# Moving the clamp and the last factor product of a group-norm, channel-norm and gate kernel from VectorE to GpSimd, with a new order on GpSimd

## The chip, the cores and the metric

The kernel runs on one core of a Trainium2 chip. The time is that of one launch on the device, in microseconds; three runs of the kernel before gave 1960.15, 1960.63 and 1963.23, a median of 1960.63. TensorE (PE) multiplies matrices into PSUM, VectorE (DVE) and ScalarE (ACT) work elementwise on SBUF and PSUM, GpSimd (POOL) elementwise on SBUF, and SyncE (SP) starts the loads. "us" is microseconds.

## The reference

The input `x` is 8 x 128 channels x 256 x 256 pixels in float32. Cut to what is computed:

```python
g = group_norm(x)                       # 32 groups of 4 channels; over the group's channels and all pixels, eps 1e-5
u = mean(g, channels); s = sqrt(var(g, channels, ddof=1))       # one value per pixel
n = (g - u) / (s + 1e-6)
n = einsum('bchw,oc->bohw', n, W) + b   # 128 x 128 matrix over the channels
out = x + g * n
```

## The kernel before, in words

**Layout and tiles.** The 128 channels are the partitions. A batch is 65536 pixels, cut into 64 slots of 1024 pixels (512 KB). Subtracting the channel mean is folded into the centred and turned matrix `w_t`. Since a group's mean and variance run over a whole batch, each batch is read first for its statistics; 33 of its 64 slots stay in SBUF from then on (`tiles`, 49 buffers), the other 31 are loaded a second time ("stream"). All of slots 41 to 63 but none of slots 0 to 10 are among the second loads.

**Stages.** The program has a first stage without output (statistics of batch 0) and then one period of 64 steps for each batch. In step t of a period, PE, DVE, ACT and POOL each do the parts below for slots that lag behind t, and the statistics of the next batch run in between, so that the periods join without a gap. Every engine walks the same steps in a program order that is written out by hand; semaphores tie them.

- **Normalise, POOL L441** (`norm`): one step ahead, `(x - mean) * inv_std`, in place. It waits for a streamed slot's load.
- **Squares, ACT L524**, then **sums, PE L722**: sums over the channels of the tile and of its squares, 32 matmuls a slot. Four slots (a "set") share one accumulator of 128 x 128 sums; there are 16 sets a batch, 128 in all.
- **Once per set**, a chain on 128x128 values turns the sums into the factor 1/(s + eps). In step t = 4 of the set (its first slot is 0): ACT squares the sum (L540, `sum_sq`), DVE forms `var` (L651) and clamps and scales it (L655, `max(var, 1e-30) / 127`). In step 5: ACT root, root + eps and root squared (L527, L529, L530), DVE reciprocal (L663, `approx`), POOL three products (L485, L459, L461) that correct the reciprocal for the error of the root. In step 6: DVE makes the last product (L667, `factor = (miss - 2) * approx`); the factor is split into three bf16 pieces by ACT L533, POOL L466 (`split_first`), ACT L536, POOL L471 (`split_second`).
- **Spread, PE L708**: from step 7 on, one slot a step, the factor is laid out over all partitions in PSUM (`factor_ps`, a single buffer).
- **Scale, DVE L632**: normalised tile times factor, eight steps behind. **Project, PE L734**: `w_t` times that, into one of two PSUM buffers.
- **Gate, DVE L645**: `(proj + shift) * tile`, in place, nine steps behind; **finish, POOL L452** (`finish`) adds the mean in the same step, and ACT starts the store one step later (L548).
- **Statistics of the next batch:** 24 slots go to DVE (two `bn_stats` each, L676 and L677) and 40 to ACT (two passes with an accumulator each, L509), over steps 0 to 57. DVE has places for its slots in the last step of each set only, mostly two slots there, in some sets one.
- **Group scalars, `gn_scalars`, L580 to L618:** in steps 59, 61 and 62, DVE turns the statistics into the scalars of the next batch, in small instructions of one or two columns, each of which waits for the one before.

**Order on each engine, inside one step.** DVE: scale, reciprocal, last factor product, gate, `var` and clamp, statistics, group scalars. POOL: normalise, first split, the three products, finish, second split. ACT: squares, the root group, the piece copies with one statistics pass between them, one statistics pass and then `sum_sq` (`SUM_SQ_AFTER = 1`), the remaining passes, the store. PE: spread, project, sums. SP: loads in the order of a planner that spaces the 95 loads of a batch 0.62 steps apart; each waits until its buffer's last user is done, and for 33 kept and all streamed buffers that is a store.

Of the kernel before, what the change touches and what calls it, by code (L numbers as in the profile page):

```python
# [8 lines left out]
ALU = mybir.AluOpType  # L9
# [3 lines left out]
P = 128  # L13
# [3 lines left out]
TINY = 1e-30  # L17
# [19 lines left out]
LAG_VAR = SPLIT  # L37
# [151 lines left out]
def norm_gate_kernel(nc, x, w, bias, const, pick, ident, out):  # L189
# [23 lines left out]
    with ExitStack() as ctx:  # L213
# [87 lines left out]
        miss_squared = sem("miss_squared")  # L301
        factor_done = sem("factor_done")
# [5 lines left out]
        SUM_SQ_AFTER = 1  # L308
# [118 lines left out]
        def _(pool):  # L427
# [27 lines left out]
            def correct(done):  # L455

                pool.wait_ge(approx_done, done)
                pool.wait_ge(miss_done, done)
                nc.gpsimd.tensor_tensor(miss[:, :], miss[:, :], approx[:, :], ALU.mult).then_inc(miss_scaled, 1)  # L459
                pool.wait_ge(miss_scaled, done)  # L460
                nc.gpsimd.tensor_tensor(miss[:, :], miss[:, :], approx[:, :], ALU.mult).then_inc(miss_squared, 1)  # L461

# [11 lines left out]
            def period(b, own, before, nxt):  # L474
                for step in steps(own, before, nxt):
                    root_of = set_behind(step, LAG_ROOT, b, own, before)
                    fit_of = set_behind(step, LAG_FIT, b, own, before)
                    if (s := behind(step, -NORM_LEAD, own, before, nxt)) is not None:
                        norm(b, step, s, own)
                    if fit_of is not None:  # L480
                        split_first(fit_of)
# [7 lines left out]
                    if fit_of is not None:  # L489
                        split_second(fit_of, step)  # L490
# [62 lines left out]
        def _(dve):  # L553
# [10 lines left out]
            def gn_scalars(n, part, of):  # L564
# [11 lines left out]
                if part == 0:  # L576
# [9 lines left out]
                    then(nc.vector.scalar_tensor_tensor(out=cell(5), in0=cell(4), scalar=cell(4), in1=cell(1),  # L586
                                                        op0=ALU.mult, op1=ALU.add))
                    then(nc.vector.scalar_tensor_tensor(out=cell(4), in0=cell(4), scalar=bn_part, in1=cell(2),
                                                        op0=ALU.mult, op1=ALU.subtract))
                    then(nc.vector.scalar_tensor_tensor(out=cell(5), in0=cell(5), scalar=bn_part, in1=cell(3),  # L590
                                                        op0=ALU.mult, op1=ALU.add))

                    then(nc.vector.scalar_tensor_tensor(out=cell(5), in0=cell(4), scalar=cell(4), in1=cell(5),
                                                        op0=ALU.mult, op1=ALU.subtract))
                    then(nc.vector.tensor_scalar(cell(6), cell(4), pivot_of(of), None, ALU.add))
                elif part == 1:
# [3 lines left out]
                    then(nc.vector.scalar_tensor_tensor(out=cell(7), in0=cell(7), scalar=cell(7), in1=cell(5),  # L600
                                                        op0=ALU.mult, op1=ALU.subtract))
# [3 lines left out]
                else:  # L605
# [3 lines left out]
                    then(nc.vector.scalar_tensor_tensor(out=cell(11), in0=cell(8), scalar=cell(10), in1=cell(9),  # L609
                                                        op0=ALU.mult, op1=ALU.add))  # L610
# [10 lines left out]
            def period(b, own, before, nxt):  # L621
                of = plan if own else first_plan
                for step in steps(own, before, nxt):
# [24 lines left out]
                    def var_of_sums(ready):  # L648
# [5 lines left out]
                        dve.wait_ge(var_sum_done, ready)  # L654
                        nc.vector.tensor_scalar(var[:, :], var[:, :], TINY, 1.0 / (P - 1), ALU.max, ALU.mult)\  # L655
                            .then_inc(var_done, 1)
# [7 lines left out]
                    if (ready := set_behind(step, LAG_FIT, b, own, before)) is not None:  # L664

                        dve.wait_ge(miss_squared, ready)
                        nc.vector.scalar_tensor_tensor(out=factor[:, :], in0=miss[:, :], scalar=-2.0, in1=approx[:, :],  # L667
                                                       op0=ALU.add, op1=ALU.mult).then_inc(factor_done, 1)
# [112 lines left out]
```

## Time and profile before

| | |
|---|---|
| median of 3 runs | 1960.63 us |
| the profiled execution: its own time / its span | 1957.16 us / 1955.4 us |
| granted TensorE clock | 0.992 |
| DVE busy | 1803.2 us (92%) |
| PE busy | 1713.4 us (88%) |
| POOL, ACT busy | 1460.6 us (75%), 1440.7 us (74%) |
| DMA | 671.63 MB, mean 343 GB/s |

The span runs from the first to the last instruction. The first stage ends at 97.5 us, when POOL takes over batch 0's scalars; the eighth and last takeover is at 1711.5 us, so a period with statistics for a next batch takes (1711.5 - 97.5) / 7 = 230.6 us on average. Durations of neighbouring instructions on one engine overlap a little, since the next one begins before the last one has left the pipeline; from start to start is what one costs in a busy row of them.

### The profile page before, as it was taken

What the parts mean: (1) busy time and instruction counts of PE and PEld (TensorE: products, weight loads), DVE (VectorE), ACT (ScalarE), POOL (GpSimd) and SP (SyncE); (2) the same over time, 40 slices, a digit from 0 to 9 for tenths busy, and PEclk for the clock granted to TensorE, in tenths of its full rate; (3) what the DMA queues carried; (4) which work ended last, traced back from release to release, by engine and by line L of the source; (5) the groups of instructions that cost most, each with busy time, mean ns of one, the idle gap of its engine ahead of it and who ended that gap; (6) DMA issues with size and microseconds to landing.
All of it is one profiled execution on the core that took longest, in us unless ns stands there. A gap on an engine that the chain in (4) does not pass through costs nothing.

```text
span 1955.4 us, 67613 instructions
## 1 busy us (share of the span) xinstructions
PE 1713.4 (88%) x28706; PEld 922.9 (47%) x28706; DVE 1803.2 (92%) x2120; ACT 1440.7 (74%) x2498; POOL 1460.6 (75%) x1684
## 2 busy tenths in 40 slices
PE   0079997999889998999989999899988999899997
PEld 0045554555445554455545554455544555455553
DVE  5669999999999998999989998999989999898988
ACT  5598885888768885788858888588876888544442
POOL 0077877878778886788868787787877888688885
PEclk9989999999999999999999999999999999999999
DMA  9989998999989998999989999899998999854775
GB/s 379 390 308 337 388 377 291 402 378 377 337 293 415 372 385 322 338 396 373 387 303 378 372 385 350 304 406 373 380 346 310 401 364 384 315 196 185 270 258 218
DMA packets 184188, 671.63 MB, mean 343 GB/s; under 512 B 20688, under 2 KB 21072, under 8 KB 183888
## 3 DMA queue, kind: packets, MB, share of 16 engines
q1 hardware_dynamic: 110160, 398.85, 55.0%
q10 hardware_dynamic: 73728, 268.47, 34.6%
q8 instruction: 227, 3.72, 0.7%
q14 instruction: 73, 0.60, 0.1%
HBM read 398.80 MB, written 268.44 MB: 341 GB/s over the span
## 4 chain that ended last, share of the span: by engine, by line
PE 47%; DVE 27%; issue 9%; DMA 9%; POOL 3%; SPq 2%; ACT 2%; POOLq 0%; ACTq 0%; DVEq 0%
PE proj_ps L734 28%; PE sums_ps L722 10%; DVE scaled L632 9%; PE factor_ps L708 9%; DMA tiles<-x 6%; DVE tiles L645 6%; DVE bn L676 4%; DVE bn L677 4%; DMA out<-tiles 3%; SPq L408 2%; POOL tiles L441 1%; POOL tiles L452 1%; DVE var L651 1%; ACT unused L509 1%; DVE gn L580 1%
## 5 line engine op out<-in xcount | busy, mean ns | idle before, releaser
L734 PE MATMUL proj_ps<-scaled,w_t 128*32 128x512 f32 x8192 | 992.3, 602 | 0.1
L452 POOL TENSOR_SCALAR tiles<-tiles,out_shift 128x1024 f32<-128x1024 f32 x512 | 576.8, 1127 | 228.6 <-DVE tiles L645 214.9
L645 DVE SCALAR_TENSOR_TENSOR tiles<-proj_ps,gate_shift,tiles 128x1024 f32<-128x1024 f32 x512 | 643.2, 1256 | 46.4 <-PE proj_ps L734 46.0
L441 POOL TENSOR_SCALAR tiles<-tiles,norm_scalars 128x1024 f32<-128x1024 f32 x512 | 618.6, 1208 | 58.0 <-DMA tiles<-x 57.2
L509 ACT ACTIVATE unused<-tiles,bn 128x1024 uint8<-128x1024 f32 x560 | 636.5, 1137 | 2.5 <-issue 1.7
L632 DVE TENSOR_TENSOR scaled<-tiles,factor_ps 128x1024 f32<-128x1024 f32 x512 | 618.4, 1208 | 6.1 <-PE factor_ps L708 3.8
L524 ACT ACTIVATE squares<-tiles 128x1024 f32<-128x1024 f32 x512 | 539.0, 1053 | 99.1 <-POOL tiles L441 74.2
L708 PE MATMUL factor_ps<-pieces,pick_sb 128*128 128x128 bf16 x4096 | 319.8, 221 | 130.5 <-DVE scaled L632 111.5
L722 PEld LDWEIGHTS sums_ps<-tiles,const_sb 128*32 128x32 f32 x8192 | 245.6, 111 | 317.9 <-issue 283.7
L734 PEld LDWEIGHTS proj_ps<-scaled,w_t 128*32 128x32 f32 x8192 | 214.7, 109 | 365.0 <-issue 311.5
L708 PEld LDWEIGHTS factor_ps<-pieces,pick_sb 128*128 128x128 bf16 x4096 | 232.5, 98 | 245.8 <-DVE scaled L632 164.5
L722 PE MATMUL sums_ps<-tiles,const_sb 128*32 128x128 f32 x8192 | 320.1, 274 | 11.9 <-ACT squares L524 11.9
L722 PE MATMUL sums_ps<-squares,const_sb 128*32 128x128 f32 x8192 | 319.7, 274 | 0.0
L722 PEld LDWEIGHTS sums_ps<-squares,const_sb 128*32 128x32 f32 x8192 | 235.8, 111 | 0.3
L533 ACT ACTIVATE piece<-sum_sq,const_sb 128x128 bf16<-128x128 f32 x128 | 51.7, 404 | 155.6 <-DVE sum_sq L667 155.6
L663 DVE RECIPROCAL approx<-approx 128x128 f32<-128x128 f32 x128 | 120.6, 942 | 15.4 <-ACT approx L529 15.4
L655 DVE TENSOR_SCALAR var<-var 128x128 f32<-128x128 f32 x128 | 123.3, 963 | 4.4
L676 DVE BATCH_NORM_STATS2 bn<-tiles 128x6 f32<-128x512 f32 x168 | 114.5, 682 | 0.0
L677 DVE BATCH_NORM_STATS2 bn<-tiles 128x6 f32<-128x512 f32 x168 | 113.7, 677 | 0.0
L459 POOL TENSOR_TENSOR miss<-miss,approx 128x128 f32<-128x128 f32 x128 | 59.1, 462 | 68.2 <-DVE approx L663 66.2
L527 ACT ACTIVATE root<-var 128x128 f32<-128x128 f32 x128 | 39.7, 310 | 92.3 <-DVE var L655 91.6
L509 ACT ACTIVATION_READ_ACCUMULATOR unused<-tiles,bn 128x1 f32 x560 | 106.0, 189 | 0.0
(56 smaller groups left out, 679.9 us busy)
## 6 DMA issues: line engine op xcount, KB each, us to landing
tiles<-x SPq DMA_DIRECT2D x760, 512.0 KB, 9.7
out<-tiles ACTq DMA_DIRECT2D x512, 512.0 KB, 6.9
const_sb<-const SPq DMA_DIRECT2D x1, 193.5 KB, 2.3
scaled<-w SPq DMA_DIRECT2D x1, 64.0 KB, 2.1
scaled<-ident SPq DMA_DIRECT2D x1, 64.0 KB, 2.1
pick_sb<-pick SPq DMA_DIRECT2D x1, 8.0 KB, 2.2
bias_sb<-bias SPq DMA_DIRECT2D x1, 0.5 KB, 2.3
```

Of the source, the lines that this page charges most:

```text
L441: nc.gpsimd.tensor_scalar(place(s), place(s), norm_scalars[:, 0:1], norm_scalars[:, 1:2], ALU.add, ALU.mult).then_inc(normed, 1)
L452: nc.gpsimd.tensor_scalar(place(s), place(s), 1.0, out_shift[:, 0:1], ALU.mult, ALU.add).then_inc(finished, 1)
L509: nc.scalar.activation(unused[:, which, :], data, (ACT.Identity, ACT.Square)[which], bias=pivot_of(of), scale=-1.0, accum_out=act_sums[:, ...
L524: nc.scalar.activation(squares[:, step % 2, :], place(step), ACT.Square).then_inc(squared, 1)
L632: nc.vector.tensor_tensor(scaled[:, s % 2, :], place(s), factor_ps[:, :], ALU.mult)\
L645: nc.vector.scalar_tensor_tensor(out=place(s), in0=proj_ps[:, s % 2, :], scalar=gate_shift[:, 0:1], in1=place(s), op0=ALU.add, op1=ALU.mul ...
L655: nc.vector.tensor_scalar(var[:, :], var[:, :], TINY, 1.0 / (P - 1), ALU.max, ALU.mult)\
L676: nc.vector.bn_stats(bn_of(of)[:, j, :], data[:, 0:BANK])
L677: nc.vector.bn_stats(bn_of(of)[:, j + 1, :], data[:, BANK:SLOT]).then_inc(bn_done, 1)
L708: mm = nc.tensor.matmul(factor_ps[:, chunk(h, t)], pick_sb[:, j:j + 1].to_broadcast([P, P]), pieces[:, s // SPLIT % 2, :], start=True, sto ...
L722: mm = nc.tensor.matmul(sums_of(s)[32 * t:32 * t + 32, which, :], rows, data[:, chunk(h, t)], start=(which == 0 and k == 0), stop=(which = ...
L734: mm = nc.tensor.matmul(proj_ps[q:q + 32, s % 2, h:h + BANK], w_t[:, q:q + 32], scaled[:, s % 2, h:h + BANK], start=True, stop=True)
```

## The change

It moves two 128x128 instructions of each set from DVE to POOL, and reorders POOL's step.

- The clamp L655 becomes a POOL `tensor_scalar` (`clamp`), after normalise in step 4; it waits for `var_sum_done` of DVE.
- The last factor product L667 becomes two POOL instructions at the end of `correct`: `miss * 1.0 - 2.0` and then the product with `approx`. They stand in step 5 instead of step 6.
- POOL's order in a step becomes: normalise, clamp, second split, products, finish, first split. The first split is issued at the end of step 5, where it was after normalise in step 6; the second split comes after normalise in step 6, where it was after finish.
- `SUM_SQ_AFTER` goes from 1 to 0: ACT squares the sum before its first statistics pass of the step, not after it.
- Six one-column `scalar_tensor_tensor` of `gn_scalars` become `tensor_scalar` with two column operands.

No instruction of PE, no load and no store is changed, nor the order of ACT beyond that constant.

```diff
-        SUM_SQ_AFTER = 1
+        SUM_SQ_AFTER = 0
...
                 nc.gpsimd.tensor_tensor(miss[:, :], miss[:, :], approx[:, :], ALU.mult).then_inc(miss_squared, 1)
+                pool.wait_ge(miss_squared, done)
+                nc.gpsimd.tensor_scalar(miss[:, :], miss[:, :], 1.0, -2.0, ALU.mult, ALU.add).then_inc(miss_shifted, 1)
+                pool.wait_ge(miss_shifted, done)
+                nc.gpsimd.tensor_tensor(factor[:, :], miss[:, :], approx[:, :], ALU.mult).then_inc(factor_done, 1)
+
+            def clamp(done):
+
+                pool.wait_ge(var_sum_done, done)
+                nc.gpsimd.tensor_scalar(var[:, :], var[:, :], TINY, 1.0 / (P - 1), ALU.max, ALU.mult).then_inc(var_done, 1)
...
                     if (s := behind(step, -NORM_LEAD, own, before, nxt)) is not None:
                         norm(b, step, s, own)
+                    if var_of is not None:
+                        clamp(var_of)
                     if fit_of is not None:
-                        split_first(fit_of)
+                        split_second(fit_of, step)
                     if root_of is not None:
...
                     if (s := behind(step, LAG_OUT, own, before)) is not None:
                         finish(b, step, s, before)
-                    if fit_of is not None:
-                        split_second(fit_of, step)
+                    if root_of is not None:
+                        split_first(root_of)
...
-                    then(nc.vector.scalar_tensor_tensor(out=cell(5), in0=cell(4), scalar=cell(4), in1=cell(1),
-                                                        op0=ALU.mult, op1=ALU.add))
+                    then(nc.vector.tensor_scalar(cell(5), cell(4), cell(4), cell(1), ALU.mult, ALU.add))
...
                         nc.vector.scalar_tensor_tensor(out=var[:, :], in0=sum_sq[:, :], scalar=-1.0 / P,
                                                        in1=sums_of(step - LAG_VAR)[:, 1, :], op0=ALU.mult, op1=ALU.add)\
                             .then_inc(var_sum_done, 1)
-                        dve.wait_ge(var_sum_done, ready)
-                        nc.vector.tensor_scalar(var[:, :], var[:, :], TINY, 1.0 / (P - 1), ALU.max, ALU.mult)\
-                            .then_inc(var_done, 1)
...
-                    if (ready := set_behind(step, LAG_FIT, b, own, before)) is not None:
-
-                        dve.wait_ge(miss_squared, ready)
-                        nc.vector.scalar_tensor_tensor(out=factor[:, :], in0=miss[:, :], scalar=-2.0, in1=approx[:, :],
-                                                       op0=ALU.add, op1=ALU.mult).then_inc(factor_done, 1)
```

The other five column forms (L588, L590, L593, L600, L609) are changed in the same way as the one shown (L586).

## Rows read from the trace of the kernel before

**Rows 1.** The page: busy times, and the chain that ended last

```profile
PE 1713.4 (88%) x28706; PEld 922.9 (47%) x28706; DVE 1803.2 (92%) x2120; ACT 1440.7 (74%) x2498; POOL 1460.6 (75%) x1684
PE 47%; DVE 27%; issue 9%; DMA 9%; POOL 3%; SPq 2%; ACT 2%; POOLq 0%; ACTq 0%; DVEq 0%
```

**Rows 2.** Timeline of DVE: `var` at sets' starts in batch 2 and the last

```profile
571.19 0.28 DVE L651 SCALAR_TENSOR_TENSOR var<-sum_sq,sums_ps 128x128 f32<-128x128 f32 x1
738.00 0.28 DVE L651 SCALAR_TENSOR_TENSOR var<-sum_sq,sums_ps 128x128 f32<-128x128 f32 x1
803.79 0.28 DVE L651 SCALAR_TENSOR_TENSOR var<-sum_sq,sums_ps 128x128 f32<-128x128 f32 x1
1729.66 0.28 DVE L651 SCALAR_TENSOR_TENSOR var<-sum_sq,sums_ps 128x128 f32<-128x128 f32 x1
1887.10 0.28 DVE L651 SCALAR_TENSOR_TENSOR var<-sum_sq,sums_ps 128x128 f32<-128x128 f32 x1
```

**Rows 3.** Timeline of DVE: one set of four steps with two statistics slots

```profile
654.63 0.28 DVE L651 SCALAR_TENSOR_TENSOR var<-sum_sq,sums_ps 128x128 f32<-128x128 f32 x1
654.95 1.07 DVE L655 TENSOR_SCALAR var<-var 128x128 f32<-128x128 f32 x1
655.94 1.21 DVE L632 TENSOR_TENSOR scaled<-tiles,factor_ps 128x1024 f32<-128x1024 f32 x1
657.07 0.94 DVE L663 RECIPROCAL approx<-approx 128x128 f32<-128x128 f32 x1
...
660.16 0.32 DVE L667 SCALAR_TENSOR_TENSOR sum_sq<-miss,approx 128x128 f32<-128x128 f32 x1
660.40 1.27 DVE L645 SCALAR_TENSOR_TENSOR tiles<-proj_ps,gate_shift,tiles 128x1024 f32<-128x1024 f32 x1
...
668.91 0.28 DVE L651 SCALAR_TENSOR_TENSOR var<-sum_sq,sums_ps 128x128 f32<-128x128 f32 x1
```

**Rows 4.** Lines taken alone: ns min/median/max, first and last start

```profile
L655 DVE TENSOR_SCALAR var<-var x128: 226/1074/1087, 111.4 to 1929.0; 128x128 f32<-128x128 f32 x128
L600 DVE SCALAR_TENSOR_TENSOR gn<-gn x8: 219/1072/1073, 94.5 to 1704.4; 128x1 f32<-128x1 f32 x8
L609 DVE SCALAR_TENSOR_TENSOR gn<-gn x8: 219/714/792, 96.2 to 1709.6; 128x1 f32<-128x1 f32 x8
L586 DVE SCALAR_TENSOR_TENSOR gn<-gn x8: 219/876/877, 92.3 to 1695.4; 128x1 f32<-128x1 f32 x8
L585 DVE TENSOR_SCALAR gn<-gn,bn x7: 213/214/215, 303.4 to 1695.2; 128x1 f32<-128x1 f32 x7
L584 DVE TENSOR_SCALAR gn<-gn x8: 170/1099/1121, 91.9 to 1694.1; 128x2 f32<-128x2 f32 x8
L435 POOL COPY norm_scalars<-new_scalars x8: 186/186/186, 97.5 to 1711.5; 128x2 f32<-128x2 f32 x8
```

**Rows 5.** Timeline of POOL in the set of rows 3

```profile
654.82 1.12 POOL L452 TENSOR_SCALAR tiles<-tiles,out_shift 128x1024 f32<-128x1024 f32 x1 [2.17 <-DVE tiles L645]
655.93 1.21 POOL L441 TENSOR_SCALAR tiles<-tiles,norm_scalars 128x1024 f32<-128x1024 f32 x1
657.09 0.47 POOL L485 TENSOR_TENSOR miss<-var,miss 128x128 f32<-128x128 f32 x1
658.09 0.47 POOL L459 TENSOR_TENSOR miss<-miss,approx 128x128 f32<-128x128 f32 x1 [0.53 <-DVE approx L663]
658.63 0.46 POOL L461 TENSOR_TENSOR miss<-miss,approx 128x128 f32<-128x128 f32 x1
```

**Rows 6.** Windows: length, busy us of PE, PEld, DVE, ACT, POOL; clock, DMA share, GB/s

```profile
0.00:90.00 90.00, 0.77 (x2) 0.50 (x2) 55.58 (x89) 54.61 (x90) 0.21 (x4) 1.00 0.99 393
566.50:740.50 174.00, 164.83 (x2795) 88.62 (x2792) 170.25 (x196) 150.64 (x267) 140.54 (x161) 1.00 1.00 385
595.50:624.50 29.00, 27.97 (x471) 14.77 (x467) 28.14 (x34) 25.69 (x46) 24.58 (x29) 1.00 1.03 417
1730.00:1880.00 150.00, 150.00 (x2568) 81.29 (x2560) 136.22 (x140) 71.69 (x116) 130.41 (x151) 1.00 0.60 227
```

**Rows 7.** Waits in batch 2 (552 to 784 us): total, times, longest

```profile
ACT piece L533 <- DVE sum_sq L667: 18.0, 16, 3.8
PE factor_ps L708 <- DVE scaled L632: 14.1, 23, 2.2
POOL tiles L441 <- DMA tiles<-x: 8.5, 5, 3.3
PE factor_ps L708 <- POOL pieces L471: 4.8, 2, 3.2
DVE var L651 <- ACT sum_sq L540: 1.5, 4, 0.7
```

More of the change, by code:

```diff
@@ L301, in norm_gate_kernel @@
         miss_squared = sem("miss_squared")
+        miss_shifted = sem("miss_shifted")
         factor_done = sem("factor_done")
@@ L475, in period @@
                 for step in steps(own, before, nxt):
+                    var_of = set_behind(step, LAG_VAR, b, own, before)
                     root_of = set_behind(step, LAG_ROOT, b, own, before)
@@ L585, in gn_scalars @@
                     then(nc.vector.tensor_scalar(cell(4), cell(0), pivot_of(of), None, ALU.subtract))
-                    then(nc.vector.scalar_tensor_tensor(out=cell(5), in0=cell(4), scalar=cell(4), in1=cell(1),
-                                                        op0=ALU.mult, op1=ALU.add))
[L588 to L594, printed above, removed]
+                    then(nc.vector.tensor_scalar(cell(5), cell(4), cell(4), cell(1), ALU.mult, ALU.add))
+                    then(nc.vector.tensor_scalar(cell(4), cell(4), bn_part, cell(2), ALU.mult, ALU.subtract))
+                    then(nc.vector.tensor_scalar(cell(5), cell(5), bn_part, cell(3), ALU.mult, ALU.add))
+                    then(nc.vector.tensor_scalar(cell(5), cell(4), cell(4), cell(5), ALU.mult, ALU.subtract))
                     then(nc.vector.tensor_scalar(cell(6), cell(4), pivot_of(of), None, ALU.add))
@@ L599, in gn_scalars @@
                     then(nc.vector.tensor_scalar(cell(7), cell(6), small_ps[:, 0:1], None, ALU.subtract))
-                    then(nc.vector.scalar_tensor_tensor(out=cell(7), in0=cell(7), scalar=cell(7), in1=cell(5),
-                                                        op0=ALU.mult, op1=ALU.subtract))
+                    then(nc.vector.tensor_scalar(cell(7), cell(7), cell(7), cell(5), ALU.mult, ALU.subtract))
                 elif part == 2:
@@ L607, in gn_scalars @@
                     then(nc.vector.reciprocal(cell(10), cell(9)))
-                    then(nc.vector.scalar_tensor_tensor(out=cell(11), in0=cell(8), scalar=cell(10), in1=cell(9),
-                                                        op0=ALU.mult, op1=ALU.add))
+                    then(nc.vector.tensor_scalar(cell(11), cell(8), cell(10), cell(9), ALU.mult, ALU.add))
                     then(nc.vector.tensor_scalar(cell(11), cell(11), 0.5, None, ALU.mult))
```

## The prediction

> **What bounds the kernel now.** I read the busy times and the chain of waits first [rows 1]. DVE is busy for 92% of the span, PE for 88%, and together they hold 74% of the chain; no engine is free enough to say at once which one sets the pace. So I then followed one instruction that comes once per set, DVE's `var`, through the timeline and took the distance from one set to the next [rows 2]. In the last batch, which has no statistics for a next one, 12 sets take 1887.10 - 1729.66 = 157.44 us, 13.12 us each, and PE is busy for 150 of 150 us there, DVE for only 136.2 [rows 6]. That is PE's own pace, 3.28 us a step. In batch 2 the same 12 sets take 738.00 - 571.19 = 166.81 us, 13.90 each, and the last four 803.79 - 738.00 = 65.79 us.
>
> The timeline of DVE shows why the earlier batches are slower [rows 3]. This set takes 668.91 - 654.63 = 14.28 us with DVE in an almost unbroken row of work, and PE waits for DVE's scale, 14.1 us in the batch [rows 7]. DVE's row holds a clamp of 1.07 us on 128x128 values. Its durations lie between 0.226 and 1.087 us with a median of 1.074 [rows 4], and the one shown ends at 656.02, just as POOL's finish, which had begun at 654.82 for 1.12 us, ends at 655.94 [rows 3, 5]. The clamp mostly waits for a POOL instruction that is under way. The same is seen on one-column instructions: L600, L586 and L609 take 0.22 us at best and 1.07, 0.88 and 0.71 in the median [rows 4]. In the main part of a batch DVE is thus the limit, PE is right behind it, and the DMA queues are a third: share 1.00 at 385 GB/s over 174 us [rows 6].
>
> **The change, part by part, for a batch with statistics (seven of eight).**
>
> *Clamp and product leave DVE.* From start to start the clamp costs 655.94 - 654.95 = 0.99 us and the product 660.40 - 660.16 = 0.24 [rows 3], 1.23 us a set. The heavy set of 14.28 us would come to 13.05, just under PE's 13.12. So the 12 sets can gain at most 166.81 - 157.44 = 9.4 us, since PE takes over as the bound at once; the other four can gain 4 x 1.23 = 4.9.
>
> *Column forms.* L600, L586 and L609 fall to what a one-column `tensor_scalar` with a column operand takes, 0.214 us in all of its seven executions (L585): 0.86 + 0.66 + 0.50 = 2.0 us a batch, on DVE alone and late in the batch, where PE has to wait for it. L588, L590 and L593 count nothing, since they seldom wait. A row speaks against this: L584, a `tensor_scalar` of two columns, takes 1.10 us in the median [rows 4]. If the new ones wait like it, the 2.0 are lost. I take 2.0, because L585 has one column, as they do. (The Trainium skill, SBUF — State Buffer, section "Who interferes with whom", says that `tensor_scalar` can enter a two-port mode that locks out GpSimd and is blocked by it, and that two SBUF inputs also contend. By its list of operations alone, without the operands, this term would be 0 and the sum 14 us higher. The trace agrees with it for L584 and not for L585.)
>
> *POOL takes on three instructions.* The product costs what the others do, 658.63 - 658.09 = 0.54 us. Clamp and shift are one-input forms of 128 columns, which no row shows. Below: an eighth of finish's 655.93 - 654.82 = 1.11 us, 0.14. Above: the two-input 0.46. Between a two-column copy of 0.19 and 1.11 at 1024 [rows 4, 5] lies 0.19 + 126 x 0.92 / 1022 = 0.30, which I take, an estimate. The sum is 1.2 us a set with a semaphore gap (0.8 to 1.6). POOL is busy 130.41 us in 150, or 11.4 in 13.12 [rows 6], and comes to 12.6 (12.2 to 13.0), still under PE's 13.12, but with half a microsecond left where it had 1.7. The cost is nothing while that cover holds; if it is gone, see the last rival.
>
> *The clamp's wait on POOL.* It waits for `var`, and finish is queued behind it. Finish already waits for the gate that stands just ahead of `var`, 2.17 us in this set [rows 5], so the wait adds `var` and clamp, 0.6 us, once a set. The root chain behind it gets earlier: clamp's end moves from 656.02 to about 655.3. It could get later by up to one normalise (1.2 us) where POOL is late; then the reciprocal, which DVE reaches one scale (1.13 us) after `var`, waits, and the gate behind it.
>
> *Order and splits.* The products now sit before finish with 0.84 us more ahead of it, so one finish and one store a set start that much later; the buffer has a step of slack for that. The first split is issued a step earlier, the second split ahead of finish, so PE's wait for the pieces (4.8 us, in two instances) can shrink or, since normalise now stands right behind a wait for ACT's copy, turn into a late normalise. I count both as 0 (-2 to +2 a batch). ACT's wait for the factor is 18.0 us over 16 sets [rows 7], slack that covers this.
>
> *`SUM_SQ_AFTER`.* DVE waits 1.5 us a batch for `sum_sq` [rows 7]. At most that is gained; ACT may idle for PE where it ran a pass before. Taken as 0.
>
> *DMA.* Nothing is added, but the same bytes have to come sooner. 174 us at 385 GB/s are 67.0 MB. At the 393 GB/s of the load-only first 90 us that takes 170.5 us, 3.5 less; at the best stretch, 417 over 29 us [rows 6], 160.7, or 13.3 less. So the 12 sets gain between 3.5 (slower rate) and 9.4 (PE). Neither end is nearer to the rows, since the stretch itself holds both kinds of rate, so I take the middle, 6. What the loads owe is paid in the last four sets, where all slots are streamed and normalise already waits 8.5 us for them; there I take half of 4.9 + 2.0, 3.5.
>
> *Elsewhere.* The first stage is loads at a share of 0.99, gain 0. The last batch already runs at PE's pace and gains 0 (up to 5 us worse, if POOL slips by 0.3 a set).
>
> The sum is 7 x (6 + 3.5) = 66.5 off the profiled execution's own 1957.2, 1890.7. The median of the runs lies 3.5 above that execution, so the forecast is 1894 us.
>
> **The rivals.**
>
> *PE's floor is reached.* The loads keep up, and each batch gains 9.4 + 6.9 = 16.3: 7 x 16.3 = 114, or 1847 us. For it speaks that DVE's heavy set comes out at 13.05; against it that four engines and the DMA all lie within a few per cent of 13.12 us and wait for each other in order. (The Trainium skill, HBM Reference, section "Specifications (TRN2)", gives about 425 GB/s for a core that streams alone. By that the 67.0 MB take 158 us and this rival would be the forecast. The rows show 417 for 29 us and 385 for 174.)
>
> *The loads take it back.* If 390 GB/s is all that this mixture reaches, the 12 sets gain 2, and of the last four only 1 is left, because waits for streamed slots grow: 7 x 3 = 21, or 1940 us. For it speak the share of 1.00 and the 8.5 us of waits, against it the 417.
>
> *POOL becomes the bound, slower than before.* Everything on POOL stands in one order, so a wait at the head (clamp for `var`, products for the reciprocal, 0.53 today [rows 5], both splits for ACT's copies) holds back finish and normalise. The seven batches run at 14.54 us a set on average in batch 2 (232.6 / 16), the last at 13.12. With x us a set everywhere the change is 112 (x - 14.54) + 16 (x - 13.12), zero at x = 14.36. That needs 1.7 us of waits on top of 12.6. At x = 14.5 it is +18 us, 1979. Against it speaks that 1.2 us of added work fill 1.7 of slack, and that most waits stand where POOL would otherwise idle.
>
> **How the numbers follow.** The forecast has 0.56, PE's floor 0.14, loads 0.17, POOL 0.09, and that gains and waits cancel 0.04. About 0.2% (4 us) is what a measurement of this kernel can tell from none. Faster is 0.56 + 0.14 + 0.17 = 0.87, the same 0.04, slower 0.09. The forecast's own range is 1865 to 1925. The range reaches to 1942, over the rival of the loads, and down to 1858, most of the way to PE's floor; it leaves out POOL's 0.09 and some 0.1 below.
>
> **What the profile after would show.** Right: L651 at 13.3 to 13.5 us apart in the 12 sets of a middle batch; clamp on POOL at 0.3 us, all alike; the one-column forms at 0.21; DVE busy about 1640 us (1803 - 128 x 1.23 - 7 x 2); POOL about 1610 (1460.6 + 128 x 1.2), at 85%; DMA above 395 GB/s in the 12 sets and longer waits of normalise for loads late in a batch. Wrong: a POOL instruction of 128 columns above 0.5 us; the reciprocal waiting for ACT more than 0.5 us a set; sets of the last batch above 13.4 us; PE waiting for pieces in most sets; or 13.12 in all 12 sets, in which case the loads were no limit.

## The result, and the profile after

The changed kernel takes 1931.41 us in the median of four runs (1927.35 to 1935.11) against 1960.72 of the kernel before, a ratio of 0.986 with a 95% interval of 0.983 to 0.989. It is faster by 29 us, 1.4%, and the interval is clear of 1; I had forecast 66. The profiled execution is the slowest of the four, 1935.11 us with a span of 1933.3, against 1957.16 and 1955.4.

The page of the changed kernel, busy times and the chain that ended last, as in [rows 1]:

```profile
PE 1714.7 (89%) x28706; PEld 923.1 (48%) x28706; DVE 1646.0 (85%) x1864; ACT 1441.0 (75%) x2498; POOL 1631.2 (84%) x2068
PE 33%; POOL 22%; DVE 18%; issue 10%; ACT 8%; DMA 6%; SPq 2%; ACTq 0%; POOLq 0%; DVEq 0%
```

DVE lost 157 us of work, nearly what was forecast, and the span lost 22. POOL and ACT are in the chain now, with 22% and 8% where they had 3% and 2%. So work went away from DVE, and waiting came in its place.

Timeline of DVE in the changed kernel, `var` (now L658) at the same places as [rows 2]:

```profile
566.14 0.28 DVE L658 SCALAR_TENSOR_TENSOR var<-sum_sq,sums_ps 128x128 f32<-128x128 f32 x1
733.26 0.28 DVE L658 SCALAR_TENSOR_TENSOR var<-sum_sq,sums_ps 128x128 f32<-128x128 f32 x1
795.49 0.28 DVE L658 SCALAR_TENSOR_TENSOR var<-sum_sq,sums_ps 128x128 f32<-128x128 f32 x1
1707.53 0.28 DVE L658 SCALAR_TENSOR_TENSOR var<-sum_sq,sums_ps 128x128 f32<-128x128 f32 x1
1866.83 0.28 DVE L658 SCALAR_TENSOR_TENSOR var<-sum_sq,sums_ps 128x128 f32<-128x128 f32 x1
```

The 12 sets take 167.12 us where they took 166.81: nothing was gained in the main part of a batch. The last four take 62.23 where they took 65.79, and that is where the time came from. In the mean over batches 1 to 6 the last four gained 4.0 us a batch, where I had forecast 3.5, and the 12 sets lost 0.3, where I had forecast a gain of 6. In the last batch 12 sets take 159.30 us, 13.28 each, where PE's pace had given 13.12.

The waits of the changed kernel over the whole run (total, times, longest):

```profile
DVE approx L667 <- ACT approx L542: 134.6, 122, 4.2
ACT piece L546 <- POOL sum_sq L466: 126.5, 119, 2.8
PE factor_ps L707 <- DVE scaled L639: 89.3, 104, 3.0
POOL tiles L442 <- DMA tiles<-x: 23.5, 20, 3.1
PE factor_ps L707 <- POOL pieces L481: 13.9, 41, 2.4
```

DVE waits 134.6 us at the reciprocal for root + eps, 1.05 us a set. In the kernel before that wait was 15.4 us in all. The wait of normalise for loads, on which I had put a part of the sum and which I expected to grow, is 23.5 us, and had been 57.2. Most of what it lost is in the set of steps 52 to 55, in which it was 3.39 us a batch before and is 0.39 now (mean over batches 1 to 6).

Two lines of the changed kernel taken alone, POOL's clamp and POOL's shift (ns min/median/max):

```profile
L471 POOL TENSOR_SCALAR var<-var x128: 639/640/643, 110.9 to 1908.3; 128x128 f32<-128x128 f32 x128
L464 POOL TENSOR_SCALAR miss<-miss x128: 298/299/303, 115.4 to 1911.8; 128x128 f32<-128x128 f32 x128
```

The shift costs the 0.30 us that I had estimated for both. The clamp has the same shape but a maximum in it, and costs 0.64, above my upper bound of 0.46.

Timeline of DVE in a set with two statistics slots, which answers to [rows 3]:

```profile
649.25 0.27 DVE L658 SCALAR_TENSOR_TENSOR var<-sum_sq,sums_ps 128x128 f32<-128x128 f32 x1
649.44 1.21 DVE L639 TENSOR_TENSOR scaled<-tiles,factor_ps 128x1024 f32<-128x1024 f32 x1
651.70 0.95 DVE L667 RECIPROCAL approx<-approx 128x128 f32<-128x128 f32 x1 [1.04 <-ACT approx L542]
...
663.38 0.28 DVE L658 SCALAR_TENSOR_TENSOR var<-sum_sq,sums_ps 128x128 f32<-128x128 f32 x1
```

ACT in the same stretch:

```profile
648.85 1.14 ACT L522 ACTIVATE unused<-tiles,bn 128x1024 uint8<-128x1024 f32 x1
649.89 0.20 ACT L522 ACTIVATION_READ_ACCUMULATOR unused<-tiles,bn 128x1 f32 x1
649.99 1.05 ACT L537 ACTIVATE squares<-tiles 128x1024 f32<-128x1024 f32 x1
650.93 0.30 ACT L540 ACTIVATE root<-var 128x128 f32<-128x128 f32 x1
651.27 0.40 ACT L542 ACTIVATE approx<-root,const_sb 128x128 f32<-128x128 f32 x1
```

And POOL's clamp there:

```profile
649.61 0.64 POOL L471 TENSOR_SCALAR var<-var 128x128 f32<-128x128 f32 x1 [0.97 <-DVE var L658]
...
663.74 0.64 POOL L471 TENSOR_SCALAR var<-var 128x128 f32<-128x128 f32 x1 [0.91 <-DVE var L658]
```

DVE is done with scale about 650.66 and stands until 651.70. The clamp ends at 650.25, ACT is in squares until 651.04, root begins at 650.93 and root + eps is there at 651.67. Before, the scale began only when the clamp had ended, and so covered the root chain; now it begins with the clamp and is over before the root has begun. POOL's row from clamp to clamp is 14.13 us with 0.91 of waiting. The other 13.2 us are more than PE's 13.12, though POOL is busy for 12.72 of them only; the rest are gaps between its 16 instructions that are too short to be listed as waits.

There is a second thing in this set, and it was there before as well. PE's spreads around the step with two statistics slots, in the kernel before (L708):

```profile
646.20 0.62 PE L708 MATMUL factor_ps<-pieces,pick_sb 128*128 128x128 bf16 x8
649.48 0.62 PE L708 MATMUL factor_ps<-pieces,pick_sb 128*128 128x128 bf16 x8
653.58 0.62 PE L708 MATMUL factor_ps<-pieces,pick_sb 128*128 128x128 bf16 x8 [0.76 <-DVE scaled L632]
657.20 0.62 PE L708 MATMUL factor_ps<-pieces,pick_sb 128*128 128x128 bf16 x8 [0.27 <-DVE scaled L632]
```

In the changed kernel (L707):

```profile
640.81 0.62 PE L707 MATMUL factor_ps<-pieces,pick_sb 128*128 128x128 bf16 x8
644.13 0.62 PE L707 MATMUL factor_ps<-pieces,pick_sb 128*128 128x128 bf16 x8
648.19 0.62 PE L707 MATMUL factor_ps<-pieces,pick_sb 128*128 128x128 bf16 x8 [0.71 <-DVE scaled L639]
651.47 0.62 PE L707 MATMUL factor_ps<-pieces,pick_sb 128*128 128x128 bf16 x8
```

A step is 3.28 us. Before, two steps were long, 4.10 and 3.62. Now one is, 4.06, while the other is 3.28: the second was the clamp's, the first was not. DVE in that step of the changed kernel:

```profile
643.35 1.28 DVE L652 SCALAR_TENSOR_TENSOR tiles<-proj_ps,gate_shift,tiles 128x1024 f32<-128x1024 f32 x1 [0.28 <-PE proj_ps L733]
644.55 0.68 DVE L675 BATCH_NORM_STATS2 bn<-tiles 128x6 f32<-128x512 f32 x1
...
646.34 0.67 DVE L676 BATCH_NORM_STATS2 bn<-tiles 128x6 f32<-128x512 f32 x1
646.93 1.20 DVE L639 TENSOR_TENSOR scaled<-tiles,factor_ps 128x1024 f32<-128x1024 f32 x1
```

It is a loop: DVE's gate waits for PE's project (0.28 us here), then come gate (1.20), two slots (2.38) and scale (1.2), and only then, at 648.19, may PE spread again. From the gate's start to that spread are 4.84 us. PE's spread before it came 0.78 us after the gate's start, at 644.13, and 4.84 - 0.78 is the step of 4.06. DVE can't run ahead through this loop, since it starts with a wait for PE. In batch 2 the kernel before has eight steps of 4.10 and eight of 3.62 in the 12 sets, 8 x 0.82 + 8 x 0.34 = 9.3 us of the 9.4 over PE's pace. In the changed kernel the eight steps with two slots take 3.84 to 4.10, the 3.62 are gone, and other steps have grown instead, to as much as 4.24.

### The profile page after: what moved, and what is told of

Its sections match the earlier page's. It is cut to its first block, busy times and chain, and to the rows that moved or that the text cites. A ratio compares the mean times of both kernels' runs of the same rounds, so it can differ in the third digit from the quotient of the medians.

```text
span 1933.3 us, 67741 instructions
## 1 busy us (share of the span) xinstructions
PE 1714.7 (89%) x28706; PEld 923.1 (48%) x28706; DVE 1646.0 (85%) x1864; ACT 1441.0 (75%) x2498; POOL 1631.2 (84%) x2068
## 4 chain that ended last, share of the span: by engine, by line
PE 33%; POOL 22%; DVE 18%; issue 10%; ACT 8%; DMA 6%; SPq 2%; ACTq 0%; POOLq 0%; DVEq 0%
PE proj_ps L733 20%; POOL tiles L442 7%; POOL tiles L453 7%; PE sums_ps L721 7%; PE factor_ps L707 6%; DVE scaled L639 6%; ACT unused L522 4%; DVE tiles L652 4%; DMA tiles<-x 3%; DVE bn L675 3%; DVE bn L676 3%; ACT squares L537 2%; SPq L409 2%; DMA out<-tiles 2%; POOL var L471 2%
## 5 line engine op out<-in xcount | busy, mean ns | idle before, releaser
L442 POOL TENSOR_SCALAR tiles<-tiles,norm_scalars 128x1024 f32<-128x1024 f32 x512 | 616.5, 1204 | 24.7 <-DMA tiles<-x 23.5
L707 PE MATMUL factor_ps<-pieces,pick_sb 128*128 128x128 bf16 x4096 | 318.1, 221 | 106.9 <-DVE scaled L639 89.3
L707 PEld LDWEIGHTS factor_ps<-pieces,pick_sb 128*128 128x128 bf16 x4096 | 231.9, 98 | 223.4 <-DVE scaled L639 120.7
L667 DVE RECIPROCAL approx<-approx 128x128 f32<-128x128 f32 x128 | 121.9, 953 | 134.6 <-ACT approx L542 134.6
L471 POOL TENSOR_SCALAR var<-var 128x128 f32<-128x128 f32 x128 | 81.9, 640 | 92.5 <-DVE var L658 88.3
```

What stands on the lines that cost most here:

```text
L442: nc.gpsimd.tensor_scalar(place(s), place(s), norm_scalars[:, 0:1], norm_scalars[:, 1:2], ALU.add, ALU.mult).then_inc(normed, 1)
L667: nc.vector.reciprocal(approx[:, :], approx[:, :]).then_inc(approx_done, 1)
L707: mm = nc.tensor.matmul(factor_ps[:, chunk(h, t)], pick_sb[:, j:j + 1].to_broadcast([P, P]), pieces[:, s // SPLIT % 2, :], start=True, sto ...
```

## The experiments

Four theories. **A:** the root chain is late, and DVE stands at the reciprocal. **B:** POOL's row is the bound. **C:** the step with two statistics slots is a loop of its own. **D:** what was gained comes from the new order of the splits. Besides the ratio to the kernel before in the same session (four runs of each kernel, ten of the column forms and of the clamp alone; 95% interval) the table has the mean over batches 1 to 6 of the profiled execution: the 12 sets, then the sets of steps 52 to 55, 56 to 59, 60 to 63, and the one across the boundary, worked out from the starts of `var` on DVE; and 12 sets of the last batch.

| kernel | median us | ratio, interval | 12 sets | last four sets | last batch |
|---|---|---|---|---|---|
| before | 1960.7 | | 166.8 | 15.4, 18.1, 16.4, 15.1 | 157.4 |
| changed | 1931.4 | 0.986 (0.983 to 0.989) | 167.1 | 13.2, 18.6, 14.9, 14.3 | 159.3 |
| column forms only | 1955.0 | 0.998 (0.996 to 0.999) | 166.8 | 15.2, 17.9, 16.1, 15.1 | 157.4 |
| clamp only, on POOL | 1963.3 | 1.002 (1.000 to 1.003) | 167.2 | 15.4, 18.4, 16.7, 14.3 | 157.7 |
| changed, clamp on DVE | 1942.8 | 0.992 (0.989 to 0.994) | 167.8 | 13.4, 19.6, 14.6, 15.1 | 157.4 |
| changed, old split order | 2016.2 | 1.029 (1.027 to 1.031) | 174.1 | 14.7, 18.7, 16.6, 14.4 | 166.7 |
| changed, no maximum | 1921.5 | 0.982 (0.980 to 0.984) | 165.9 | 13.6, 18.8, 14.8, 14.3 | 157.4 |
| changed, reciprocal after gate | 1922.6 | 0.982 (0.980 to 0.984) | 165.3 | 14.6, 17.5, 15.1, 14.3 | 159.3 |
| changed, root before squares | 1922.2 | 0.980 (0.978 to 0.982) | 165.3 | 15.2, 17.7, 15.2, 14.3 | 159.0 |
| before, one slot a step | 1949.7 | 0.995 (0.994 to 0.997) | 164.8 | 15.5, 17.8, 17.3, 14.8 | 157.4 |
| changed, one slot a step | 1926.4 | 0.984 (0.982 to 0.987) | 166.5 | 13.4, 18.0, 14.7, 13.7 | 159.4 |
| both: one slot, reciprocal after gate | 1894.6 | 0.966 (0.964 to 0.968) | 161.5 | 14.4, 17.9, 14.8, 13.7 | 159.3 |
| both, no maximum | 1887.6 | 0.963 (0.959 to 0.967) | 160.4 | 14.9, 17.4, 14.7, 13.7 | 157.7 |
| both, no maximum, root before squares | 1884.2 | 0.961 (0.959 to 0.963) | 157.9 | 17.0, 16.6, 15.6, 13.7 | 157.7 |

The kernels without the maximum leave a part of the clamp out: a variance that rounding made negative is no longer raised. They are there to tell what bounds the time. Of the last four sets the first scatters most from batch to batch, in the kernel before between 14.3 and 16.7 us.

**The parts alone.** The column forms in the kernel before, six replacements like this one:

```diff
-                    then(nc.vector.scalar_tensor_tensor(out=cell(5), in0=cell(4), scalar=cell(4), in1=cell(1),
-                                                        op0=ALU.mult, op1=ALU.add))
+                    then(nc.vector.tensor_scalar(cell(5), cell(4), cell(4), cell(1), ALU.mult, ALU.add))
```

> The kernel before with the six one-column forms alone. The changed kernel's forms take 0.27 us or 0.22 each, 1.52 us a batch where the six took 2.9 in the mean, so DVE is free 1.4 us earlier in each of seven batches. If DVE sets the pace at the batch boundary: 7 x 1.4 = 10 us less, about 1950 us. If the loads of the streamed slots set it there: no change, 1959 to 1961.

It came to 1955.0, 4 us less than the kernel before in the same session (1959.0), with an interval of 1 to 8. The forms take 0.27 or 0.21 us each without waiting, and about half of the 1.4 us a batch reaches the end.

The clamp alone, in the kernel before:

```diff
-                        dve.wait_ge(var_sum_done, ready)
-                        nc.vector.tensor_scalar(var[:, :], var[:, :], TINY, 1.0 / (P - 1), ALU.max, ALU.mult)\
-                            .then_inc(var_done, 1)
...
                         norm(b, step, s, own)
+                    if (var_of := set_behind(step, LAG_VAR, b, own, before)) is not None:
+                        clamp(var_of)
```

> The kernel before with the clamp alone moved to POOL (0.64 us there), in POOL's order of before. DVE loses 0.99 us a set and gains a wait at the reciprocal of about the same size, 0.8 to 1.2 us. The 12 sets come to 165 to 168 us and the time to 1950 to 1965 us. If the wait were covered by POOL's idle time, as I forecast, the time would be 1910 to 1925.

1963.3 us, 167.2 in the 12 sets: the clamp's time leaves DVE and comes back as waiting. My forecast of this part is refuted. The waiting is in two places. DVE's wait at the reciprocal rises from 15.4 to 82.0 us over the run, 0.64 us a set, less than the 0.8 to 1.2 that I wrote. And the whole chain is later, so that PE's wait for the pieces rises from 18.8 to 55.5 us.

The reverse, the clamp back on DVE in the changed kernel:

```diff
+                        dve.wait_ge(var_sum_done, ready)
+                        nc.vector.tensor_scalar(var[:, :], var[:, :], TINY, 1.0 / (P - 1), ALU.max, ALU.mult)\
+                            .then_inc(var_done, 1)
...
-                    if var_of is not None:
-                        clamp(var_of)
```

> The changed kernel with the clamp back on DVE behind var, everything else as changed. Theory A (the late chain var, clamp, root, root + eps makes DVE wait 1.05 us a set at the reciprocal): that wait falls to about 0.1 us, the clamp takes its 0.99 us back, the two nearly cancel, and the time stays near the changed kernel's, 1925 to 1940 us. Theory B (POOL's row is full and sets the pace): POOL is relieved of 0.64 us a set plus its wait for var, and the time falls by 7 x 16 x 0.6 = 67 us, to about 1865.

1942.8, a little above theory A's range and far from B's 1865: relieving POOL of its clamp doesn't help, at least not where DVE has to do it. Moving the clamp to POOL is worth 11 us in the changed kernel, where it cost 3 in the kernel before.

**Theory D: the order.**

```diff
                     if fit_of is not None:
-                        split_second(fit_of, step)
+                        split_first(fit_of)
...
-                    if root_of is not None:
-                        split_first(root_of)
+                    if fit_of is not None:
+                        split_second(fit_of, step)
```

> The changed kernel with the splits where they were: first split after normalise in step 6, second split after finish. Theory D (what the change gained is gained by the new order, in the set of steps 52 to 55, which takes 15.4 us before and 13.2 after, because the pieces no longer stand behind a normalise and a finish that are late by their loads): that set goes back to 15 us or more, the one of steps 60 to 63 to 16, and the time rises by 7 x 3 to 1950 us. If the gain is the work taken off DVE, the time stays within 1925 to 1940.

2016.2 us, a direction as expected and a size far beyond. Set 52 to 55 goes back to 14.7, less than I wrote, set 60 to 63 to 16.6, but the 12 sets rise by 7 us too. The waits of this kernel over the whole run show why:

```profile
ACT piece L549 <- POOL sum_sq L476: 180.8, 127, 2.5
DVE approx L667 <- ACT approx L542: 155.2, 122, 4.7
PE factor_ps L707 <- POOL pieces L481: 111.7, 121, 3.1
```

PE waits 111.7 us for the pieces, at nearly every set, where it waits 13.9 in the changed kernel. Over the 96 sets of batches 1 to 6 the pieces are there 8.6 us after the clamp's start in the median of the changed kernel, and 9.7 here. The early first split pays for the longer chain. It can stand in step 5 only because the last product does, so these two parts belong together.

That the order by itself carries the gain in set 52 to 55 isn't shown. The kernel with the clamp on DVE has the new order and 13.4 us there, but the kernels further down have it too, with up to 17.0. What that set's length goes with, in all fourteen kernels, is normalise's wait for streamed slots in it. Eight of them, means over batches 1 to 6:

| kernel | set 52 to 55, us | normalise's wait for loads in it, us |
|---|---|---|
| changed | 13.2 | 0.39 |
| changed, clamp on DVE | 13.4 | 1.19 |
| changed, old split order | 14.7 | 1.51 |
| changed, reciprocal after gate | 14.6 | 1.77 |
| both, no maximum | 14.9 | 2.29 |
| changed, root before squares | 15.2 | 2.35 |
| before | 15.4 | 3.39 |
| both, no maximum, root before squares | 17.0 | 3.38 |

Why the loads are there earlier in the changed kernel, whose 12 sets are no faster, stays open.

**Theory A: the chain to the reciprocal.** Three edits shorten or cover it. The reciprocal behind gate:

```diff
-                    if (ready := set_behind(step, LAG_ROOT, b, own, before)) is not None:
-                        dve.wait_ge(root_eps_done, ready)
-                        nc.vector.reciprocal(approx[:, :], approx[:, :]).then_inc(approx_done, 1)
                     gate()
+                    if (ready := set_behind(step, LAG_ROOT, b, own, before)) is not None:
+                        dve.wait_ge(root_eps_done, ready)
+                        nc.vector.reciprocal(approx[:, :], approx[:, :]).then_inc(approx_done, 1)
```

> The changed kernel with DVE's gate of the step ahead of the reciprocal, nothing else. Theory A (DVE stands still for the root chain): the gate's 1.2 us cover the 1.05 us of waiting, DVE's wait for root + eps falls from 134.6 us to below 30, the 12 sets of a batch from 167.1 to 158 to 162 us, the time to 1875 to 1900 us. Theory B (POOL is the bound): the products start no earlier, POOL's row is as full as before, and the time stays within 1925 to 1940.

The wait falls from 134.6 to 20.2 us as theory A had it, and the time by 9 us only, not by 31 to 56. DVE's standing still was true but not by itself the bound: its wait for PE's project rises from 75.0 to 131.0 us instead. PE's spreads in the set with two slots of this kernel:

```profile
652.57 0.62 PE L707 MATMUL factor_ps<-pieces,pick_sb 128*128 128x128 bf16 x8
656.11 0.62 PE L707 MATMUL factor_ps<-pieces,pick_sb 128*128 128x128 bf16 x8 [0.19 <-POOL pieces L481]
659.96 0.62 PE L707 MATMUL factor_ps<-pieces,pick_sb 128*128 128x128 bf16 x8 [0.50 <-DVE scaled L639]
```

The steps are 3.54 and 3.85 us, the second before DVE's scale again. This led to theory C.

The clamp without its maximum:

```diff
-                nc.gpsimd.tensor_scalar(var[:, :], var[:, :], TINY, 1.0 / (P - 1), ALU.max, ALU.mult).then_inc(var_done, 1)
+                nc.gpsimd.tensor_scalar(var[:, :], var[:, :], 1.0 / (P - 1), TINY, ALU.mult, ALU.add).then_inc(var_done, 1)
```

> The changed kernel with POOL's clamp as a multiply and an add (var / 127 + 1e-30); the maximum is left out. It should take 0.30 us like the shift, where the clamp takes 0.64. Theory A: the chain is 0.34 us shorter in each set, DVE's wait falls by up to 0.34 x 128 = 43 us, the time to 1890 to 1905 us where DVE has no other slack. If ACT is busy with a statistics pass when the clamp ends anyway, the gain is smaller, 1915 to 1930. Theory B: POOL is relieved by 0.34 us a set, 7 x 16 x 0.34 = 38 us, the same size, but DVE's wait would not be what shrinks.

It takes 0.298 us, DVE's wait falls by 32 us, and the time by 10, the smaller gain for which a busy ACT was the condition. The edit relieves POOL as well, so that it is the shorter wait that speaks for theory A here, and not the time. The last batch returns from 159.3 to 157.4, which the edits that leave POOL's work alone don't bring (159.3 with the reciprocal after gate, 159.0 with the root before squares): there POOL's row was the bound, and 0.34 us less of it suffices.

ACT's root group ahead of squares in step 5, the two blocks exchanged:

```diff
-                    if own:
...
-                        nc.scalar.activation(squares[:, step % 2, :], place(step), ACT.Square).then_inc(squared, 1)
                     if (done := set_behind(step, LAG_ROOT, b, own, before)) is not None:
...
                         nc.scalar.activation(miss[:, :], root[:, :], ACT.Square).then_inc(root_sq_done, 1)
+                    if own:
...
+                        nc.scalar.activation(squares[:, step % 2, :], place(step), ACT.Square).then_inc(squared, 1)
```

> The changed kernel with ACT's root group ahead of squares in step 5. Theory A: where the clamp's result is there before ACT starts on squares (1.05 us), root starts up to 1 us earlier and DVE's wait at the reciprocal falls from 134.6 us to 60 to 100; where it is not, ACT now waits and squares come later. Time 1915 to 1935 us. Theory B (POOL's row is the bound): unchanged, since POOL's work is.

DVE's wait falls to 82.9 us, the time to 1922.2, both within theory A's numbers.

**Theory C: the step with two slots.**

```diff
-    plan = plan_statistics(slots, STATS_DVE, STATS_UNTIL, range(3, SPLIT))
+    plan = plan_statistics(slots, STATS_DVE, STATS_UNTIL, range(2, SPLIT))
```

> The changed kernel, but DVE's statistics slots of a later batch may start in the last two steps of a set, so that no step holds two. Theory C (the step with two slots is a loop of its own: PE's project, gate 1.2, two slots 2.4, scale 1.2, PE's spread, 4.06 us from spread to spread where PE needs 3.28, before and after the change alike, 4.10 and 4.06): no step is over 3.3 for that reason any more, the 12 sets fall from 167.1 us to 158 to 162, the time by 7 x (5 to 9) to 1870 to 1897 us. Theory A alone (the late root chain sets the pace): the reciprocal waits as before and the time stays within 1920 to 1935.

The edit starts one of the two slots a step earlier, and the planner of the loads, which reads the same plan, moves with it.

The time stays at 1926.4, where theory A alone had it. But the loop itself is gone, as PE's spreads show:

```profile
640.56 0.62 PE L707 MATMUL factor_ps<-pieces,pick_sb 128*128 128x128 bf16 x8
643.99 0.61 PE L707 MATMUL factor_ps<-pieces,pick_sb 128*128 128x128 bf16 x8
647.41 0.62 PE L707 MATMUL factor_ps<-pieces,pick_sb 128*128 128x128 bf16 x8
650.69 0.62 PE L707 MATMUL factor_ps<-pieces,pick_sb 128*128 128x128 bf16 x8
654.78 0.62 PE L707 MATMUL factor_ps<-pieces,pick_sb 128*128 128x128 bf16 x8 [0.75 <-DVE scaled L639]
```

The steps with a slot each take 3.43 and 3.42 us. What had been lost there is lost in the step of the reciprocal instead (4.09), and DVE's wait for root + eps grows from 134.6 to 157.9 us. The same edit in the kernel before:

> The kernel before with the same places for DVE's statistics, one slot a step. DVE's row of a set with two slots holds about 14.0 us of work there, so spreading it gains little: the 12 sets fall from 166.8 us to 163 to 166, the time to 1930 to 1955 us. If the loop through the two-slot step were all that mattered in the kernel before, the 12 sets would fall to about 158 and the time to about 1900.

1949.7 us and 164.8 in the 12 sets: with the clamp and the product on DVE, its work is the limit. In batch 2 it is busy for 162.9 of the 164.8 us.

Both edits together, the `gate()` diff and the `range(2, SPLIT)` diff above in one kernel:

> The changed kernel with both single edits: DVE's reciprocal behind gate, and one statistics slot a step. Alone they gave 165.3 and 166.5 us for the 12 sets where the changed kernel has 167.1. Theory A + C (two waits that stand in for each other: the two-slot step and the wait at the reciprocal): together more than the sum of both, 159 to 163 us, time 1880 to 1900 us. Theory B (POOL's row of 13.28 us a set is the floor, which the changed kernel's last batch shows): not under 12 x 13.28 = 159.4 us. If the gains only add: 164.7 us, 1912 to 1920.

1894.6 us. Alone they gave 9 and 5 us, together they give 37. Each obstacle had hidden the other. The waits of this kernel over the whole run:

```profile
DVE tiles L652 <- PE proj_ps L733: 104.1, 201, 2.2
PE factor_ps L707 <- POOL pieces L481: 45.8, 58, 3.2
POOL tiles L442 <- DMA tiles<-x: 34.9, 30, 3.1
DVE approx L668 <- ACT approx L542: 33.7, 42, 2.9
```

DVE waits for PE, as it should when PE is the bound, though that alone proves little, since it was 131.0 us with the reciprocal after gate. What tells more is PE's own wait for DVE's scale: 89.3 us in the changed kernel, 57.7 with the reciprocal after gate, 74.9 with one slot a step and 22.5 here. This version computes everything the reference asks for and is faster than both kernels.

The same with the clamp's diff, the maximum left out:

> The kernel with the reciprocal behind gate and one statistics slot a step, and the maximum left out of POOL's clamp (0.30 us instead of 0.64). POOL's row falls from 13.28 to 12.94 us a set, under PE's 13.12. If POOL's row is the floor of that kernel, its 12 sets fall by up to 2 us, to 157.5 to 160; if not, by less than 0.5. Time 1870 to 1895 us.

1887.6 us, whose runs spread from 1881.5 to 1896.0: the 12 sets fall by 1.1, between the two expectations, and the last batch by 1.6 us. POOL's row is a small part of what is left.

And with ACT's two blocks exchanged as well:

> As the kernel with reciprocal behind gate, one slot a step and no maximum, and also ACT's root group ahead of squares in step 5. If ACT's lateness for root still holds DVE or POOL there, 1 to 3 us a batch less, 7 to 20 us in all; with the reciprocal behind gate I expect that it is covered: no difference beyond 4 us.

I expected no difference in the 12 sets and there is one, 160.4 to 157.9, which is PE's 157.4 but for 0.5. The total moves by 3 us only, within 4 as expected, since set 52 to 55 rises from 14.9 to 17.0. The window of one batch's 12 sets in this kernel (length, busy of PE, PEld, DVE, ACT, POOL; clock, DMA share, GB/s):

```profile
551.00:709.00 158.00, 157.77 (x2699) 85.66 (x2692) 150.59 (x162) 143.83 (x253) 147.36 (x193) 1.00 1.02 403
```

The queues carry 403 GB/s over 158 us, where [rows 6] had 385 over 174. That the late set is then held by its loads is likely: normalise waits 3.38 us for them there and PE 2.86 for the pieces, where it is 2.29 and 1.61 without the last edit. No run takes the loads away to prove it.

## Why the prediction was wrong

**The whole miss is in the 12 sets**, 6.3 us in each of batches 1 to 6. Two steps of the prediction failed there. **The first** is "the heavy set of 14.28 us would come to 13.05, just under PE's 13.12". It is a sum of DVE's work over a set. A set has four steps, each coupled to PE in both directions, and the step with two slots costs about 4.1 us of PE's time where 3.28 are needed, before and after. With up to 0.8 us in each of the eight sets with two slots among the 12, some 6 of the 9.4 us that I counted on were never the clamp's to give; the 3.62 us steps held 2.7. Spreading the slots shows it, but only together with the other edit.

**The second is "the clamp's wait on POOL"**, where I had the root chain get earlier and the reciprocal wait only where POOL is late. I compared the clamp's end with its old end, 656.02 to 655.3, and not with the moment at which DVE asks for the result. DVE's own clock had moved ahead by the same 0.99 us. The result was wanted one scale after `var` in place of one scale after the clamp, and in that one scale lie now two semaphore hops, the clamp, ACT's squares, root and add. The wait there is 1.05 us a set, where it was 0.12, and that takes up nearly all of the 0.99 that the clamp had freed. The clamp-only kernel, 1963.3, shows that nothing of it is left, though there a part goes into PE's wait for later pieces.

**The price of the clamp** was 0.30 with an upper bound of 0.46, and measured 0.64: I bounded by shape and number of inputs, and the operation matters. The three instructions together still cost what I had allowed, 1.33 us a set (170.6 / 128) for 1.2 (0.8 to 1.6), and POOL's busy time in the last batch is 12.7 us a set for 12.6. What I left out are the gaps between its instructions: its row takes 13.28 us there without one wait above 0.15, so that 0.6 us a set of small gaps were not in my comparison with PE's 13.12. The last batch lost 1.9 us over 12 sets through it. The rival of POOL as the bound was right on that batch; for the others no run relieves POOL and changes nothing else.

**The term of the loads was wrong as a cause in the 12 sets.** I let it cut the gain from 9.4 to 6. The changed kernel moves its bytes at the old pace, and with both obstacles gone the 12 sets reach 161.5 us and even 157.9. The rival of the loads gave 1940, near the measured 1931, by a mechanism that isn't at work there; that the measured time lies in my range of 1858 to 1942 is owed to that rival, and is luck. Late in a batch the loads do count, as the table of set 52 to 55 has it, but their waits fell where I had them grow, so that the 4.0 us for my 3.5 is luck too.

**The order was counted as 0 (-2 to +2 a batch)** and is far from it. Its removal from the changed kernel costs 85 us (2016.2 - 1931.4), 11 us a batch. That is what the longer chain would cost without it, and not a gain over the kernel before; no run has the order without the product's move. The changed kernel gains 2.2 us in set 52 to 55, 1.5 in set 60 to 63 and 0.8 across the boundary; putting the old order back costs 1.5 and 1.7 of the first two, while the 0.8 is there with the clamp alone and belongs to it. The 1.5 is a mean over batches of 13.9 to 18.5 us and is within their scatter.

**Smaller slips.** 1803 - 128 x 1.23 - 7 x 2 is 1632, not 1640, and the middle between 3.5 and 9.4 is 6.5, not 6; neither decides anything. Of the signs of being right, `var` at 13.3 to 13.5 us apart (13.93) and more than 395 GB/s in the 12 sets (380 over 174 us) did not come.

**Right were** the main shape of the busy times (DVE 1646 for about 1640, POOL 1631 for about 1610), that PE's 13.12 is the floor, the shift's 0.30, and that the one-column forms don't wait; four of the six are 0.27 rather than 0.21 us, and they give about 4 us in all where I had 14. `SUM_SQ_AFTER` was not tried by itself and stays open.

## What to carry to other kernels

Work taken off an engine counts only in a step where that engine's own row of work, not a loop through another engine, sets the pace: look at the distance between two starts of the bound engine step by step, not at sums over a period. When a link of a chain is moved to another engine, the engine it leaves runs ahead by just that much and asks for the chain's end earlier; compute the wait at the place where the result is read, and put cover there (here the gate ahead of the reciprocal). And where two single edits gain next to nothing, try them together before giving either up.

## What the runs showed of the hardware

GpSimd's `tensor_scalar` on 128x128 float32 took 0.64 us with a maximum and a multiply (639 to 643 ns over 128 executions) and 0.30 with a multiply and an add (297 to 301), in place and from the same tile. (The Trainium skill, GPSIMD Engine Reference, section "3.1 Elementwise — side-by-side cycle accounting", has bodies of up to two operations bound by the port at 1.03 cycles an element, by which both forms would cost the same. The trace doesn't agree for the maximum.)

On VectorE, a one-column `tensor_scalar` took 0.273 us with two column operands and 0.214 with a column and a constant, and none waited for GpSimd, where the one-column `scalar_tensor_tensor` had taken 1.07 in the median of one line. The two-column `tensor_scalar` still takes up to 1.17 us. The 128x128 `tensor_scalar` of the kernel before (the clamp) began under a running GpSimd instruction in 121 of its 128 executions, and ended 0.08 us after that instruction each time; in the other seven it took 0.226 to 0.228 us.

Loads and stores together ran at 403 GB/s over 158 us in the fastest kernel. (The Trainium skill, HBM Reference, section "Specifications (TRN2)", gives about 425 for a core alone. No run here came nearer over such a stretch, and none shows that it could not.)
